# Attention and top-2 experts on one core: score products on row halves of the array, another order of VectorE's work, a broadcast copy moved to GpSimd

## What is computed

```
q = rope(layernorm(x) @ q_w.T + q_b) * d ** -0.5     # d = 16, 16 heads
k = rope(ctx @ k_w.T + k_b);  v = ctx @ v_w.T + v_b
scores = q . k over the window of 65 keys
probs  = exp(scores - max) / sum                      # softmax over the window
x = x + (probs @ v) @ o_w.T + o_b
xn = layernorm(x)
top2 = top_k(softmax(xn @ router_w.T), 2)
for e in 8 experts:
    out += mask_e * (silu(xn @ gate.T) * (xn @ up.T)) @ down.T * mean_weight_e
x = x + out
```

## Time and profile before

| | |
|---|---|
| median of 3 runs | 502.63 us (501.22 to 503.87) |
| the profiled execution | 498.88 us, of which its span 496.9 us |
| mean granted TensorE clock | 0.961 of full speed |
| busy over the span | PE 444.2 us (89%), DVE 301.7 (61%), ACT 270.8 (54%), POOL 118.4 (24%) |
| attention stage | about 20.7 to 203 us of the span; experts from about 225 us |

### The profile page before, as it was taken

One profiled execution on the slowest core, in us unless ns is written; L12 is line 12 of the kernel. 1 busy time (PEld: TensorE's weight loads), 2 busy tenths in 40 slices (PEclk: granted clock), 3 DMA queues, 4 the chain that ended last, 5 costly groups with the idle time before them and its releaser, 6 DMA issues.

```text
span 496.9 us, 8810 instructions
## 1 busy us (share of the span) xinstructions
PE 444.2 (89%) x2747; PEld 365.4 (74%) x2747; DVE 301.7 (61%) x727; ACT 270.8 (54%) x853; POOL 118.4 (24%) x118
## 2 busy tenths in 40 slices
PE   3897999999999998309999999999999999999980
PEld 2655675656666654208999999999999999999980
DVE  3664869797887966873746646557376473663330
ACT  1286877787778687404545546455454463643330
POOL 5201014141514214530004041050320402204013
PEclk9999999999999999657999999999999999999995
DMA  7074301020202111157655546554566453213003
GB/s 237 25 209 142 135 22 52 21 64 8 62 12 57 27 41 52 41 153 265 234 160 123 163 105 164 180 98 154 133 149 201 80 168 93 30 39 38 1 1 36
DMA packets 24317, 49.36 MB, mean 99 GB/s; under 512 B 5368, under 2 KB 15160, under 8 KB 24140
## 3 DMA queue, kind: packets, MB, share of 16 engines
q10 hardware_dynamic: 7886, 26.44, 17.2%
q1 hardware_dynamic: 10238, 15.36, 10.3%
q0 software_dynamic: 6144, 6.97, 8.6%
HBM read 38.51 MB, written 12.74 MB: 103 GB/s over the span
## 4 chain that ended last, share of the span: by engine, by line
PE 73%; DVE 7%; ACT 6%; issue 4%; POOL 3%; DMA 3%; SPq 2%; ACTq 1%; POOLq 0%; DVEq 0%
PE b_o L634 9%; PE b_small L634 9%; PE b_s L621 8%; PE b_s L622 8%; PE b_s L623 8%; PE b_s L420 6%; ACT probs L749 4%; PE b_pv L443 3%; PE b_pt L621 3%; PE b_pt L623 3%; PE b_pt L622 3%; PE b_pt L429 3%; PE b_proj L474 3%; PE b_proj L498 2%; PE b_s L418 2%
## 5 line engine op out<-in xcount | busy, mean ns | idle before, releaser
L749 ACT ACTIVATE probs<-b_s,negmax 100x100 f32<-100x100 f32 x256 | 85.6, 361 | 24.1 <-DVE negmax L1003 21.2
L1191 POOL DMA_INDIRECT out<-y_sb,idnow x32 | 48.7, 1522 | 180.5 <-ACT y_sb L790 173.1
L778 ACT CAST h_hi<-h_sb 128x448 fp32r<-128x448 f32 x64 | 36.3, 567 | 86.5 <-DVE h_sb L1094 86.5
L621 PE MATMUL b_s<-x_hi,w_hi 128*128 128x448 f32 x192 | 72.2, 376 | 0.7 <-DVE x_lo L1084 0.7
L622 PE MATMUL b_s<-x_lo,w_hi 128*128 128x448 f32 x192 | 71.3, 371 | 0.0
L623 PE MATMUL b_s<-x_hi,w_lo 128*128 128x448 f32 x192 | 71.1, 370 | 0.0
L981 DVE TENSOR_TENSOR w_lo<-w_raw,w_hi 128x1024 fp32r<-128x1024 f32 x48 | 58.4, 1224 | 13.6 <-ACT w_hi L713 13.6
L1098 DVE TENSOR_TENSOR h_lo<-h_sb,h_hi 128x448 fp32r<-128x448 f32 x64 | 40.2, 628 | 40.5 <-ACT h_hi L778 40.5
L749 ACT ACTIVATION_READ_ACCUMULATOR probs<-b_s,negmax 100x1 f32 x256 | 57.1, 223 | 0.0
L420 PE MATMUL b_s<-kblk,qrot 128*100 128x400 f32 x128 | 53.7, 500 | 0.0
L1003 DVE TENSOR_REDUCE negmax<-b_s 100x4 f32<-100x400 f32 x64 | 36.2, 566 | 27.0 <-PE b_s L420 26.3
(11 more groups left out here) (131 smaller groups left out, 930.2 us busy)
## 6 DMA issues: line engine op xcount, KB each, us to landing
w_raw<-in_ffw ACTq DMA_DIRECT2D x48, 512.0 KB, 3.9
xin<-slots SPq DMA_DIRECT2D x9, 449.8 KB, 4.6
slots<-in_padrows SPq DMA_DIRECT2D x8, 449.8 KB, 4.6
kblk<-krot SPq DMA_DIRECT2D x128, 12.5 KB, 1.8
out<-x_all SPq DMA_DIRECT2D x8, 200.0 KB
ctx_all<-in_ctxT SPq DMA_DIRECT2D x1, 1200.0 KB, 6.3
x_all<-in_x SPq DMA_DIRECT2D x1, 1200.0 KB
attw<-in_wT ACTq DMA_DIRECT2D x2, 256.0 KB, 3.7
```

Of the source, the lines that this page charges most:

```text
L621: pe.matmul(o, wh[:, c, cols], x_hi[:, c, :], start=(c == 0), stop=False)
L749: m = nc.scalar.activation(probs[:, N % 3, h, :], b_s[N % 3][0:S, h * S:(h + 1) * S], ACT.Exp, bias=negmax[:, N % 4, h:h + 1], accum_out=p ...
L778: nc.scalar.copy(h_hi[:, f, :], h_sb[:, f % 2, :]).then_inc(s_hhi, 1)
L1191: G.indirect_dma_start(out, bass.IndirectOffsetOnAxis(idnow[:, n:n + 1], 0), y_sb[:, n, :], None, bounds_check=TOK + TILE - 1, oob_is_err= ...
```

## The change

The change has three parts. (1) `kblk` keeps 4 head blocks in place of 8, since heads 0 to 3 lie in rows 0 to 63 and heads 4 to 7 in rows 64 to 127. `scores` now treats two quads at once, in even slots only: two mask matmuls, then two products with 64 rows each, on the upper and on the lower half of the array's rows, into two banks. (2) Work is moved between slots: `k_project` and ACT's evacuation of it from slot 1 to 0, `q_project` from 3 to 2, `k_rotate` from 2 to 1, `q_rotate` from 5 to 6, `rows_write` from 6 to 5, `xn_stats` from 7 to 3. (3) DVE only takes the reciprocals; POOL spreads them (`spread`), in a new order of its queue. In `rows_write` two small copies become one.

```
-        kblk = att_sb("kblk", [P, 2, DC, HC, PT])
+        kblk = att_sb("kblk", [P, 2, DC, QH, PT])
...
-                        sp.dma_start(kblk[r, i % 2, c, h, :],
+                        sp.dma_start(kblk[r, i % 2, c, h % QH, :],
...
-                if N >= 3:
-                    pe.wait_ge(s_p, N - 2)
-                o = b_s[N % 3][0:S, 0:QH * S]
-                pe.matmul(o, ident_bf[0:S, 0:S], mask_bf[0:S].rearrange("p h s -> p (h s)"),
-                          start=True, stop=False)
-                pe.matmul(o, qrot[:, i % 2, 2 * c + b, :],
-                          kblk[:, i % 2, c, h:h + QH, b * S:(b + 1) * S],
-                          start=False, stop=True).then_inc(s_s, 1)
+                banks = []
+                for m in range(2):
+                    N = NQ * i + n + m
+                    if N >= 3:
+                        pe.wait_ge(s_p, N - 2)
+                    banks.append(b_s[N % 3][0:S, 0:QH * S])
+                    pe.matmul(banks[m], ident_bf[0:S, 0:S], mask_bf[0:S].rearrange("p h s -> p (h s)"),
+                              start=True, stop=False)
+                for m in range(2):
+                    r = slice(m * P // 2, (m + 1) * P // 2)
+                    pe.matmul(banks[m], qrot[r, i % 2, 2 * c + b, :],
+                              kblk[r, i % 2, c, :, b * S:(b + 1) * S],
+                              start=False, stop=True).then_inc(s_s, 1)
...
-                    if cur:
+                    if cur and n % 2 == 0:
                         scores(i, n)
...
-                    if n == 3 and nxt:
+                    if n == 2 and nxt:
                         q_project(i + 1)
...
-                    if n == (0 if i < 0 else 1) and nxt:
+                    if n == 0 and nxt:
                         k_project(i + 1)
...
             def den(r):
                 v.wait_ge(s_p, 4 * r + 4)
-                link(V.reciprocal(rden[:, r % 2, :], psums[:, r % 2, :]))
-                if r:
-                    v.wait_ge(s_rT, r)
-                V.tensor_copy(rdenx[:, :, :], bc(rden[:, r % 2, :].unsqueeze(2), [S, H, DH])).then_inc(s_rx, 1)
+                V.reciprocal(rden[:, r % 2, :], psums[:, r % 2, :]).then_inc(s_rden, 1)
...
+            def spread(r):
+                g.wait_ge(s_rden, r + 1)
+                if r:
+                    g.wait_ge(s_rT, r)
+                G.tensor_copy(rdenx[:, :, :], rden[:, r % 2, :].unsqueeze(2).to_broadcast([S, H, DH])).then_inc(s_rx, 1)
```

More of the change, by code:

```diff
@@ L268, in build @@
         s_pv = sem("s_pv")
+        s_rden = sem("s_rden")
         s_rx = sem("s_rx")
@@ L406, in scores @@
             def scores(i, n):
-                N = NQ * i + n
                 b, s = quad(n)
                 c = s * QH // HC
-                h = s * QH % HC
                 if n == 0:
@@ L928, in rows_write @@
                     v.wait_ge(s_scat[i % 2], 16 * TOPK * 2 * (i // 2))
+                V.tensor_copy(xrow[:, i % 2, :, D:RW].rearrange("p b w -> p (b w)").bitcast(I32),
+                              rows_sb[0:S, 2 * i:2 * i + 2])
                 for b in range(2):
-                    V.tensor_copy(xrow[:, i % 2, b, D:RW].bitcast(I32), rows_sb[0:S, 2 * i + b:2 * i + b + 1])
                     ins = V.tensor_scalar(xrow[:, i % 2, b, 0:D], x_all[:, 2 * i + b, :], mv2[:, b, 0:1],
@@ L1011, in _ @@
                         attend(2 * i - 1)
-                    if n == (0 if i < 0 else 2) and nxt:
+                    if n == (0 if i < 0 else 1) and nxt:
                         k_rotate(i + 1)
@@ L1020, in _ @@
                         choose_counts(i - 2)
+                    if n == 3 and i + 2 < NPAIR:
+                        xn_stats(i + 2)
                     if n == 4 and prv:
@@ L1024, in _ @@
                         den(2 * i)
+                    if n == 5 and prv:
+                        rows_write(i - 1)
                     if n == 5 and 0 <= i - 2 < NPAIR:
                         places(i - 2)
-                    if n == 5 and nxt:
-                        q_rotate(i + 1)
                     if n == 6 and cur:
                         attend(2 * i)
-                    if n == 6 and prv:
-                        rows_write(i - 1)
+                    if n == 6 and nxt:
+                        q_rotate(i + 1)
                     if n == 7 and nxt:
@@ L1036, in _ @@
                         v_write(i + 1)
-                    if n == 7 and i + 2 < NPAIR:
-                        xn_stats(i + 2)
             V.tensor_tensor(delta[:, :, :].rearrange("p k t -> p t k"),
@@ L1164, in _ @@
                 if 0 <= i - 1 < NPAIR:
+                    spread(2 * i - 1)
+                if i + 2 < NPAIR:
+                    inverse_deviation(i + 2, s_var, mv, ve, rstd, s_rstd, s_xn)
+                if 0 <= i - 1 < NPAIR:
                     inverse_deviation(i - 1, s_var2, mv2, ve2, rstd2, s_rstd2, s_xr)
+                if 0 <= i < NPAIR:
+                    spread(2 * i)
                 if 0 <= i - 2 < NPAIR:
                     scatter(i - 2)
-                if i + 2 < NPAIR:
-                    inverse_deviation(i + 2, s_var, mv, ve, rstd, s_rstd, s_xn)
             g.wait_ge(s_first, 1)
```

## The result

The changed kernel takes 518.45 us (median of 5 runs, 516.55 to 523.81) against 502.63 (5 runs now, 501.22 to 505.39): a ratio of 1.0326, interval 1.0261 to 1.0392. The profiled execution is the longest of the five, 523.81 us with a span of 520.7, 5.4 us above the median; the others have spans of 514.7 to 520.2. Its page gives PE 448.5 us busy (before 444.2), and a mean granted clock of 0.934 (0.961).

What follows compares the result with a forecast made beforehand. PE was taken to bound the kernel now, and after the change a ring through PE and DVE. Middle pairs -0.35, first pairs +3.3, end -0.6 and +1.1 sum to +3.5 us: 502.63 becomes 506.1 us, range 495 to 512.

Steps and rivals of the forecast that it cites:

- Slower: Sign of the whole kernel's change: slower 0.48, same 0.30, faster 0.22.
- the first pairs: Pairs 0 and 1: quad 0's transposes behind q_project and weight loads ahead of xn_copy start pair 2 3.3 us later.
- The price of a pair of quads: PE's masks and products for two quads: 1.29 us instead of 1.76, bounds 1.15 and 1.96.
- The rival of staggered products: Row-half products on PE run staggered or serial: +0.67 or +1.34 us a period, 510 to 514 us; chance 0.11.
- The ring: Middle pairs: dependence chain from scores(2,3) through PE and DVE to the next sets the period, 22.39 us against 22.46.
- Its parts 4.04 and 12.31: PE's slot 2 up to the logits, 4.04 us; DVE's choose to the end of q_rotate with hand-over, 12.31 us.
- The third, 6.04: PE's slots 0 and 1, from quad 0 to quad 2 of the next pair: 6.04 us, today 6.51.
- PE has 1.9 us less work and stands idle for it: PE in a middle pair: saves 1.9 us, idle ahead of quad 0 and ahead of values in slot 6.
- The end: Last pair -0.6 us, set by ACT's last exponentials; then +1.1 us from the later scatter on the way to the experts.
- POOL's copy: POOL's spread of the reciprocals: 0.5 us, just covered before PE asks for it; no cost.
- the rival of the two holding each other up: POOL's copy holds up a DVE step of slot 5 by up to 0.5 us: +2.5, 509 us; chance 0.07.
- The rival of 492 us: Ring has slack and PE sets the middle pairs' period, 20.5 us: about -10 us, 492 us; chance 0.20.

Runs made afterwards that it cites:

- 5: Kernel 1 with PE's q_project moved behind the transposes of quad 0 and the routing logits in slot 2: 511.02 us, ratio 1.0207.
- 6: 5 with DVE's q_rotate back in slot 5, ahead of the maximum of slot 6 and attend: 514.56 us, ratio 1.0264.
- 14: Kernel 1 with rows_write back in slot 6, last there, behind attend and q_rotate: 511.75 us, ratio 1.0262.
- kernel 8: 6 with rows_write back in slot 6 and xn_stats in slot 7 (DVE's old order); halves, early keys and POOL's spread kept: 522.87 us, ratio 1.0485.
- Kernel 1: Changed kernel with xn_stats(2), in pair 0 alone, back from slot 3 to slot 7: 514.65 us, ratio 1.0296.
- kernel 12: Kernel 1 with ACT's six weight loads of pair 1 spread over slots 2 to 7: 507.65 us, ratio 1.0175.
- 7: Kernel before with the row halves alone, plus repeated masks to fill PE's freed time: 512.98 us, ratio 1.025.
- 9: Kernel before with two quads started at once in even slots, but each product on all 128 rows: 508.87 us, ratio 1.0192.
- 13: Kernel 8 with POOL's scatter ahead of the reciprocal deviation, residual in slot 3, pair 1's weight loads spread over slots 2 to 7: 497.48 us, ratio 0.996.

## Why the prediction was wrong

Slower was the likeliest sign (0.48) and came true; 518.45 us lies outside 495 to 512. The sign is in part luck: the forecast's 3.5 us came for the most part from the first pairs, where the largest loss did lie, but for reasons that it hadn't counted. Two steps failed: the sum for the first pairs, which left out the wait for x, and the taking of PE's idle time as free, with no term for TensorE's level.

- *The price of a pair of quads*: 1.29 forecast, 1.32 measured. (Its lower bound of 1.15 doesn't follow from its own terms: 0.37 + 0.67 without the switches is 1.04.) The strict order of matmuls in the Trainium skill, page "TensorE: Matmul & The Clock Gate", Part 3, "The mechanism", as I had read it, would have made it 1.62; the row halves ran side by side here, as the column tiles did in the earlier trace rows. The rival of staggered products is out.
- *The ring*: 22.39 forecast, 22.89 measured. Its parts 4.04 and 12.31 measured 4.11 and 12.35. The third, 6.04, was 6.43, and 0.3 of that is the group at 132.74, which takes 0.77 to the next start where it took 0.47. Its second half waited for ACT's copy:

```profile
132.51 0.49 ACT L733 COPY probsT<-b_pt 100x400 f32<-100x400 f32 x1 [0.20 <-PE b_pt L433]
```

  The copy came 0.20 us behind the keys' evacuation, waiting for PE's transposes at 131.92, which now stand behind `k_project` in PE's queue. The prediction had looked at the evacuation alone. Over five pairs this makes +2.1 in place of -0.35, a term that was mis-sized; the other 1.7 of the 3.8 is the fall of the level in pair 3. The ring also wasn't the only one: 5, 6 and 14 show others of the same length.
- *"PE has 1.9 us less work and stands idle for it"*: it stands idle where that was foretold, 1.38 + 0.62 us (its busy time fell by 1.1 and not 1.9), and this was taken for harmless. That failed: the prediction held no term for TensorE's level. A fall costs 1.7 us in a middle pair of after, slow records make some 7.5 of the 17.0 us of the first two pairs, and in kernel 8 the level more than doubled the loss of a wait of 2.63 us.
- *The first pairs*: +3.3 forecast, +17.0 in the profiled execution, the largest error of the sum. Kernel 1 puts some 9.5 of this down to the wait for x and the slow records behind it; the prediction didn't look for it, though the diff moves `xn_stats(2)` four slots nearer to the load. Of the remaining 7.4 kernel 12 removes 3.8: the weight loads ahead of `xn_copy` and the lower level behind. The forecast had pair 1 at 1.9 longer, without the level. The last 3.6 are in pair 0, which takes 22.9 us in kernel 12 and 19.2 in before, with four waits of 0.61 to 0.67 us for ACT and products of 1.66 us; no run takes these apart.
- *The end*: -0.6 and +1.1 forecast, +2.7 measured. Kernel 14 gets 2.2 us back (53.6 to 51.4) by taking `rows_write` with its wait for POOL from ahead of `attend`, which I hadn't counted in the last pair. That this order is the whole of it isn't shown; 7 and 9 with the old order have 53.4 and 52.8 there.
- *POOL's copy*: forecast 0.5 us and covered; it takes 0.39 to 0.40. Of the two copies in the middle pair above, DVE is idle beside one, and has L930 beside the other: 0.34 us, and 0.30 away from a copy in kernel 14. So the rival of the two holding each other up has at most 0.04 us here; a longer DVE step that starts under a copy doesn't occur in that pair. But "behind it in POOL's queue" was only half the question: kernel 8 shows what stands ahead of it to matter.
- *The rival of 492 us*: the period did come down to 21.67 when the order allowed it (13), which is still not its 20.5, and the total didn't follow.

## What to carry to other kernels

An engine's freed time is worth nothing until every ring through it is shorter: list all waits that end near the same place, not the one that ends last, and expect the next at the same length. Look for what an instruction waits on when it is moved earlier, at the start of the program above all, where loads are still on their way and everything in the same queue stands behind it. And count a stall of TensorE's at more than its length: records behind it may run at half the rate, as behind the 2.63 us of kernel 8.

## What was not expected of the hardware

TensorE's level fell behind waits of 5.74, 2.57 and 2.63 us in the profiles read above, and also behind two short ones of 0.41 and 0.62 us, then in two of five equal pairs (kernel 9), while the waits of 0.62 and 1.38 us in each middle pair of after passed in four of five. Repeated masks in PE's free time (7) didn't hold the level. The wait of 1.97 us in pair 1 of before left no slow record behind. Which pattern of waits decides stays open here.
